# Masked keys as the moving operand, masked blocks filled by DMAs, and the products of a pair of windows in another order

## The reference

```python
q = (x @ wq.T + bq).reshape(B, S, H, D)      # k and v alike
loc = jnp.einsum('bnihd,bnjhd->bnihj', qw, kw) * scale
scores = scores.at[:, n_idx, :, :, n_idx, :].set(loc...)
scores = scores.at[:, gi[:, None], :, gi[None, :]].add(gsc...)
attn = jax.nn.softmax(scores, axis=-1)
out = jnp.einsum('bihj,bjhd->bihd', attn, v).reshape(B, S, HID)
x = _layernorm(x + out @ wo.T + bo)
x = _layernorm(x + ffn(x))                   # argmax of 8 logits picks one 256-64-256 network
```

## Time and profile before

| | |
|---|---|
| median of 3 runs | 444.06 us (442.19 to 445.27) |
| span of the profiled execution | 442.8 us |
| mean granted clock of TensorE | 0.989 |
| busy: PE, PEld, DVE, ACT, POOL | 405.3, 339.8, 326.1, 250.6, 220.4 us |
| row maximum of step 1, of step 5, of step 31 starts at | 39.38, 74.98, 292.66 us |

### The profile page before, as it was taken

The page is one execution under the profiler, slowest core; times in us unless marked ns, Lnnn a source line. Parts: engine busy times, 40 slices in busy tenths (PEclk is TensorE's granted clock), DMA queues, the critical chain, the costliest instruction groups (busy, mean ns, idle before and its releaser), DMA issues.

```text
span 442.8 us, 14658 instructions
## 1 busy us (share of the span) xinstructions
PE 405.3 (92%) x5747; PEld 339.8 (77%) x5747; DVE 326.1 (74%) x796; ACT 250.6 (57%) x523; POOL 220.4 (50%) x301
## 2 busy tenths in 40 slices
PE   5899799999999999999999899988798998999991
PEld 4758678888888888888888778756577887777891
DVE  6785687758757757757759888563668998899785
ACT  3424665675575575575576576676663555544421
POOL 4361343464464464464464566435733485477540
PEclk9999999999999999999999999999989999999997
DMA  8663740000000000000020000000000011011004
GB/s 240 186 199 111 240 137 4 27 25 0 24 24 0 24 24 0 24 24 0 24 72 4 25 2 3 3 1 2 0 2 2 1 49 47 0 47 49 34 15 143
DMA packets 21720, 20.34 MB, mean 46 GB/s; under 512 B 3133, under 2 KB 21682, under 8 KB 21682
## 3 DMA queue, kind: packets, MB, share of 16 engines
q1 hardware_dynamic: 16900, 15.07, 10.9%
q10 hardware_dynamic: 4782, 4.75, 3.3%
HBM read 15.41 MB, written 4.41 MB: 45 GB/s over the span
## 4 chain that ended last, share of the span: by engine, by line
PE 52%; DVE 26%; ACT 9%; issue 8%; DMA 3%; ACTq 1%; DVEq 0%; POOL 0%; POOLq 0%
DVE row_max_t L1154 10%; PE ps L1461 7%; PE ps L1737 7%; PE ps L1424 7%; PE ps L1562 5%; PE ps L1384 5%; PE ps L1415 4%; PE ps L1438 3%; PE ps L1444 3%; ACT probs L847 3%; DVE k_part L1013 2%; ACT boundsT_t L858 2%; PE ps L1406 2%; DMA rows<-in_L_attn_x_dram 2%; ACT k_part L713 2%
## 5 line engine op out<-in xcount | busy, mean ns | idle before, releaser
L847 ACT ACTIVATE probs<-ps 128x1024 f32<-128x1024 f32 x64 | 62.1, 1022 | 68.2 <-PE ps L1428 68.2
L1154 DVE TENSOR_REDUCE row_max_t<-ps 128x16 f32<-128x2048 f32 x31 | 70.9, 2287 | 3.7 <-PE ps L1415 3.6
L1737 PE MATMUL ps<-w_part,hm_part 128*128 128x256 f32 x384 | 53.8, 289 | 1.8 <-DVE hm_part L1332 1.8
L1415 PE MATMUL ps<-k_part,q_part 32*128 32x128 f32 x1584 | 51.5, 274 | 3.1 <-issue 1.5
L1415 PEld LDWEIGHTS ps<-k_part,q_part 32*128 32x128 f32 x1584 | 46.9, 186 | 9.2 <-issue 7.0
L1562 PE MATMUL ps<-xh_parts,w_part 128*128 128x512 f32 x192 | 53.8, 416 | 0.0
L557 POOL TENSOR_TENSOR q_part<-qf,q_part 128x512 fp32r<-128x512 f32 x32 | 41.0, 1281 | 25.7 <-ACT q_part L695 25.7
L599 POOL TENSOR_TENSOR attn_t<-num_t,rden_t 128x256 f32<-128x256 f32 x32 | 20.0, 624 | 64.7 <-DVE rden_t L1185 64.7
L1737 PEld LDWEIGHTS ps<-w_part,hm_part 128*128 128x128 f32 x384 | 48.2, 190 | 4.8 <-DVE hm_part L1332 2.4
L788 ACT ACTIVATE ffn_rows<-ps,b1s 128x512 f32<-128x512 f32 x32 | 22.0, 687 | 42.2 <-PE ps L1562 34.1
L1562 PEld LDWEIGHTS ps<-xh_parts,w_part 128*128 128x128 f32 x192 | 34.7, 194 | 6.5 <-issue 0.6
(11 more groups left out here) (234 smaller groups left out, 906.4 us busy)
## 6 DMA issues: line engine op xcount, KB each, us to landing
table<-rest_sums SPq DMA_DIRECT2D x4, 1088.0 KB, 6.1
xs<-in_L_attn_x_dram SPq DMA_DIRECT2D x16, 256.0 KB, 2.8
rows<-in_L_attn_x_dram ACTq DMA_DIRECT2D x4, 1024.0 KB, 8.1
out_dram<-yout SPq DMA_DIRECT2D x6, 512.0 KB, 2.9
w<-in_L_ffn_W_dram SPq DMA_DIRECT2D x2, 256.0 KB, 7.6
w<-in_L_ffn_W_dram SPq DMA_DIRECT2D x1, 512.0 KB, 4.2
out_dram<-yout SPq DMA_DIRECT2D x2, 256.0 KB, 2.6
out_dram<-yout ACTq DMA_DIRECT2D x2, 256.0 KB, 2.8
```

The costliest lines, as they stand in the source:

```text
L847: act.activation(probs[:, 2 * h:2 * h + 2, :], ps[:, 2 * h:2 * h + 2, :], ACT.Exp).then_inc(probs_ready, 1)
L1154: dve.tensor_reduce(row_max[:], ps_all, op=ALU.max, axis=AX.X).then_inc(max_ready, 1)
L1415: last = mm(ps[:, u, (2 * c + a) * P:(2 * c + a + 1) * P], q_part[x][quad(u), s, c, a, :], k_part[y][quad(u), s, c, :], start=(i == 0), st ...
L1737: mm(y, hm_part[a][:, 1 - p, f, c * P:(c + 1) * P], w2_part[b][:, f, :], start=(f == 0 and i == 0), stop=False)
```

## The change

The masked operand changes sides, and it is no longer computed but copied.

* Even and odd partitions now hold the two heads of a quadrant (weights and biases are put in that order once, at the start). `q_part` and `k_part` are unmasked; `q_apart` and `k_apart` are their masked forms, one for a pair of windows each, with the other head's partitions zero. `k_apart` lies in the tile of the expert layer (`xh_parts`) and is zeroed once by POOL.
* POOL issues two DMAs for each, one for even and one for odd partitions (64 partitions, two runs of 2 KB each): `part_keys` in odd steps, `part_queries` in even steps. There is one buffer of each, so `part_keys` waits for the scores of the pair before, and `part_queries` for its last turned scores.
* `scores(s)` now has the unmasked query stationary and both masked key blocks moving: 24 matmuls of 256 columns. The first two windows and the global tokens keep the old form (`scores_by_queries`).
* Queries are handled as keys are: high part on ACT with bias (two instructions of 128x256), low part on DVE (two). Gone are DVE's four masking instructions, ACT's 128x1024 copy and POOL's `q_low`.
* PE's products move: key product under the even row maximum, query product at the end of the even step; both halves of the values under the odd one; `turn_x` behind the odd turned scores. ACT's and DVE's parts of them move along.

The diff, cut to its core:

```diff
@@ -119,6 +119,8 @@
...
         xh_part = [xh_parts[:, :, i] for i in range(2)]
+        k_apart = xh_parts[:, 0].rearrange("p i c n -> p i (c n)").rearrange("p i (a c w n) -> p i a c w n", a=2, c=KC, w=2)
+        qg_part = xh_parts[:, 1].rearrange("p i c n -> p (i c n)")[:, 0:2 * GT].rearrange("p (i a c n) -> p i a c n", i=2, a=2, c=KC)
...
@@ -551,10 +563,20 @@
...
-            def q_low(w, s):
-                need(pool, turned_scores_in_psum, w - 3)
-                pool.wait_ge(q_high_ready, w // 2 + 1)
-                pool.tensor_tensor(q_part[1][:, s], qf[:, s % 2], q_part[0][:, s].bitcast(fp32), ALU.subtract).then_inc(q_ready, 1)
+            def part_keys(s):
...
+                for a in range(2):
+                    pool.dma_start(k_apart[a:P:2, :, a], k_part[a:P:2, :, s // 2]).then_inc(k_apart_ready, 16)
...
+            def part_queries(s):
...
+                for a in range(2):
+                    pool.dma_start(q_apart[a:P:2, :, a], q_part[a:P:2, :, s // 2]).then_inc(q_apart_ready, 16)
...
+            def first_low(w):
+                pool.wait_ge(q_high_ready, 1)
@@ -572,24 +594,34 @@
...
                 ahead, cur, pp, old, older = (live(t + k, steady) for k in (AHEAD, 0, -2, -3, -4))
+                if live(t + 1, steady) and p:
+                    pool.wait_ge(k_ready, t // 2 + 2)
+                    pool.wait_ge(scores_in_psum, t + 1)
...
                                        e_val[:, p, :].unsqueeze(2).broadcast_to([P, HEADS, VA]), ALU.mult).then_inc(rest_ready, 1)
-                if live(t + 1, steady) and (steady or t > 0):
-                    q_low(t + 1, (s + 1) % SLOTS)
+                if live(t + 1, steady) and p:
+                    if not steady and t == 1:
+                        pool.wait_ge(k_apart_zero, 1)
+                    part_keys((s + 1) % SLOTS)
...
                                        by_quad(bounds[:], 0), ALU.subtract).then_inc(bound_low_ready, 1)
+                    if p == 0 and (steady or t > 0):
+                        pool.wait_ge(q_ready, t // 2 + 1)
+                        pool.wait_ge(turned_scores_in_psum, t)
...
                                        ALU.subtract).then_inc(e_arg_ready, 1)
+                    if p == 0 and (steady or t > 0):
+                        part_queries(s)
...
@@ -635,6 +667,8 @@
...
+            pool.wait_ge(wT_in_psum, 4)
+            pool.tensor_tensor(xh_parts[:, 0].rearrange("p i c n -> p (i c n)"), zeros16[:, 0:1].broadcast_to([P, 4 * GT]), zeros16[:, 0:1].broadcast_to([P, 4 * GT]), ALU.mult).then_inc(k_apart_zero, 1)
...
@@ -723,15 +760,21 @@
...
-                need(act, turned_scores_in_psum, w - 2)
-                act.wait_ge(qf_ready, w // 2 + 1)
-                copy(q_part[0][:, s:s + 2], qf[:]).then_inc(q_high_ready, 1)
+                need(act, turned_scores_in_psum, w - 3)
+                act.wait_ge(q_in_psum, w // 2 + 1)
+                for c in range(KC):
+                    last = act.activation(q_part[:, 0, s // 2, c].rearrange("p w n -> p (w n)"), ps_xq[:, c * 2 * P:(c + 1) * 2 * P],
+                                          ACT.Identity, bias=bq_scaled[:, c:c + 1])
+                last.then_inc(q_high_ready, 1)
...
@@ -808,18 +852,14 @@
...
-                if ahead and p == 0:
-                    turned_x(t + AHEAD)
-                if cur and p == 0 and (steady or t > 0):
-                    values_of(t, s)
+                if not steady and t == 0:
+                    turned_x(AHEAD)
                 if live(t + 1, steady) and p:
-                    keys_of(t + 1, (s + 1) % SLOTS)
+                    queries_of(t + 1, (s + 1) % SLOTS)
...
                     copy(aT[:].rearrange("p c n -> p (c n)"), ps_rao[:, 0:HID]).then_inc(aT_ready, 1)
-                if live(t + 1, steady) and p:
-                    queries_of(t + 1, (s + 1) % SLOTS)
...
                     keep_onehot(0, 0)
+                if live(t + 1, steady) and p:
+                    values_of(t + 1, (s + 1) % SLOTS)
...
                     copy(x_rest[:].rearrange("p c n -> p (c n)"), ps_rao[:, 0:KC * 2 * NW]).then_inc(x_rest_ready, 1)
+                if ahead and p == 0:
+                    keys_of(t + AHEAD, (s + AHEAD) % SLOTS)
+                if live(t + 3, steady) and p:
+                    turned_x(t + 3)
...
@@ -995,44 +1043,53 @@
...
-            def queries_of(w):
...
-                need(dve, q_ready, w)
-                dve.wait_ge(q_in_psum, w // 2 + 1)
+            def first_queries():
...
+                dve.wait_ge(q_in_psum, 1)
...
                     for c in range(KC):
-                        last = dve.scalar_tensor_tensor(qf[:, k, c, :, :],
+                        last = dve.scalar_tensor_tensor(qf[:, :, c, k, :],
                                                         ps_xq[:, (2 * c + k) * P:(2 * c + k + 1) * P].unsqueeze(1).broadcast_to([P, 2, P]),
-                                                        bq_col[:, c:c + 1], q_scale[:], ALU.add, ALU.mult)
-                last.then_inc(qf_ready, 1)
+                                                        bq_scaled[:, c:c + 1], of_half[:], ALU.add, ALU.mult)
+                last.then_inc(q_ready, 1)
...
+            def queries_of(w, s):
...
+                dve.wait_ge(q_high_ready, w // 2 + 1)
+                for c in range(KC):
+                    last = dve.scalar_tensor_tensor(q_part[:, 1, s // 2, c].rearrange("p w n -> p (w n)"), ps_xq[:, c * 2 * P:(c + 1) * 2 * P],
+                                                    bq_scaled[:, c:c + 1], q_part[:, 0, s // 2, c].rearrange("p w n -> p (w n)").bitcast(fp32),
+                                                    ALU.add, ALU.subtract)
+                last.then_inc(q_ready, 1)
...
                 for c in range(KC):
-                    last = dve.scalar_tensor_tensor(k_part[1][:, s:s + 2, c, :], ps_kv[:, c * 2 * P:(c + 1) * 2 * P].rearrange("p (w n) -> p w n", w=2),
-                                                    bk_col[:, c:c + 1], k_part[0][:, s:s + 2, c, :].bitcast(fp32), ALU.add, ALU.subtract)
+                    last = dve.scalar_tensor_tensor(k_part[:, 1, s // 2, c].rearrange("p w n -> p (w n)"), ps_kv[:, c * 2 * P:(c + 1) * 2 * P],
+                                                    bk_col[:, c:c + 1], k_part[:, 0, s // 2, c].rearrange("p w n -> p (w n)").bitcast(fp32),
+                                                    ALU.add, ALU.subtract)
...
@@ -1172,8 +1229,8 @@
...
                 early(1)
-                if ahead and p == 0:
-                    queries_of(t + AHEAD)
+                if live(t + 1, steady) and p:
+                    queries_of(t + 1, (s + 1) % SLOTS)
...
@@ -1211,10 +1268,9 @@
...
                     stack_second_bias(t - 2)
-                if not steady and t == NW - 2:
+                if not steady and t == NW - 1:
...
@@ -1406,27 +1462,37 @@
...
-            def scores(s):
+            def scores_by_queries(queries, keys_):
...
                             for u in range(UNITS):
-                                last = mm(ps[:, u, (2 * c + a) * P:(2 * c + a + 1) * P], q_part[x][quad(u), s, c, a, :],
-                                          k_part[y][quad(u), s, c, :], start=(i == 0), stop=(i == 2), tile_position=(32 * u, 0))
+                                last = mm(ps[:, u, (2 * c + a) * P:(2 * c + a + 1) * P], queries[quad(u), x, a, c, :],
+                                          keys_[quad(u), y, c, :], start=(i == 0), stop=(i == 2), tile_position=(32 * u, 0))
...
-            def turned_scores(s):
+            def both(c, u):
+                return ps[:, u, 2 * c * P:(2 * c + 2) * P].rearrange("p (a n) -> p a n", a=2)
...
+            def scores(s):
...
                         for u in range(UNITS):
-                            mm(ps[:, u, 2 * c * P:(2 * c + 2) * P], k_part[y][quad(u), s, c, :],
-                               q_part[x][quad(u), s, c, :, :].rearrange("p a n -> p (a n)"),
+                            last = mm(both(c, u), q_part[quad(u), x, s // 2, c, s % 2, :], k_apart[quad(u), y, :, c, s % 2, :],
+                                      start=(i == 0), stop=(i == 2), tile_position=(32 * u, 0))
+                return last
...
+            def turned_scores(s):
...
+                for c in range(KC):
+                    for i, (x, y) in enumerate(SPLIT):
+                        for u in range(UNITS):
@@ -1574,9 +1641,15 @@
...
                     need(pe, probs_ready, 2 * (t - 1))
-                    pe.wait_ge(q_ready, t + 1)
-                    pe.wait_ge(k_ready, t // 2 + 1)
-                    scores(s).then_inc(scores_in_psum, 1)
+                    if not steady and t == 1:
+                        pe.wait_ge(first_low_ready, 2)
+                        pe.wait_ge(k_ready, 1)
+                        scores_by_queries(q_apart[:, :, :, :, 1, :], k_part[:, :, 0, :, 1, :]).then_inc(scores_in_psum, 1)
+                    else:
+                        pe.wait_ge(q_ready, t // 2 + 1)
```

(16 more changed lines are left out.)

98 lines of the change are left out of this document (61 added, 37 removed).

## The result

The changed kernel took **450.19 us** (median of 4 runs, 448.74 to 451.91), the one before 444.66 on the same chip (442.19 to 446.3): a ratio of 1.0136, 95% interval 1.009 to 1.0181. The forecast was 441.2, on the other side. The profiled execution (451.49 us, one of the two longer ones) spans 449.4 us against 442.8.

The account below looks back on a forecast made before the run. The prediction took PE, busy 92% of the span, and its ring of handovers with DVE as the bound. Thirteen pairs (-4.3), beginning (+2.0) and end (-0.5) gave -2.8 us, so 441.2 us; range 433 to 455.

Parts of the forecast that it names:

- Scores: PE's score matmuls in each step: 24 of 256 columns in 0.86 us instead of 48 in 1.50, saving 0.64 us.
- Rival 3: Columns, not issue, decide the scores' time, so that edit frees nothing: 458 us; chance 0.05.
- Arc 2: Scores to the next turned scores: 3.49 us in both steps, 0.64 less in odd and 0.54 less in even.
- Arc 1, odd: Turned scores to scores, odd step: turn_x waits for DVE's low queries, 0.85 us more, to 5.16.
- The even arc: Turned scores to scores, even step: query product replaces key product, length kept at 4.45 us.
- POOL's issues: Four DMA issues a pair on POOL: hidden, no cost; the queries' two free up to 0.88 us each.
- Rival 1: POOL's issue of the queries' two DMAs ahead of attn is the bound: 452 us at 1.3 us each; chance 0.22.
- rival 4: The masked copies land late, each us past 4.4 costing one us a pair: 454 us; chance 0.06.
- The pairs: Window loop, steps 5 to 31: each of 13 pairs 0.33 us shorter, 4.3 us in all.
- Beginning: Zero fill of 4.9 us in POOL's queue makes PE 2.4 us late; net +2.0 us, bounds +0.5 and +3.
- End: Two casts move behind the last row maximum and hold up the routing: -0.5 us, bounds -0.9 and +0.5.
- The sum: Whole kernel: -4.3 + 2.0 - 0.5 = -2.8 us, from 444.06 to 441.2 us.

Follow-up runs that it names:

- c_dma4: Changed kernel with fill moved, casts early, square root step removed and earlier key copies; each masked copy split, four POOL issues of 128 KB for two of 256: 450.48 us.
- b_fill: Kernel before the change plus only the zero fill's work on POOL (2048 columns in two instructions, same place): 446.29 us, ratio 1.0049.
- b_take: Kernel before the change with only DVE's casts of the first token group moved from ahead of the last row maximum to behind that step's residual: 447.54 us.
- a_newton: Changed kernel without the reciprocal square root step behind the residual, six early slots a window step instead of seven: 448.16 us.
- d_turn: Changed kernel with one edit, turn_x in odd steps put behind the turned sums and the output product: 442.53 us, ratio 0.9979.

## Why the prediction was wrong, by its own steps

- **Scores: right.** 24 matmuls take 0.92 us (167.85 to 168.77) against the 0.86 forecast and the 1.50 before: 38 ns each. Rival 3 is out, and the row was the better guide. By the rule that the prediction quotes from the Trainium skill (TensorE: Matmul & The Clock Gate, Back-to-back issue gap) the same columns cost nearly the same; here they did not (1.50 and 0.92 us). The same section calls the rule that of an isolated matmul, which counts too little at few columns once weight loads are in the stream; relative to each other the two rows differ that way, though both are shorter than the rule's own sum (some 2.7 us for either, an estimate from it).
- **Arc 2: right.** 171.39 - 167.86 = 3.53 and 179.30 - 175.75 = 3.55, forecast 3.49.
- **Arc 1, odd: right in kind, too large.** Turned 162.93, scores 167.86: 4.93, forecast 5.16. It grew by 0.62 us, not 0.85; VectorE's low queries start 0.36 us behind the turned scores, not 0.49. The other odd step of a round has 3.94 before and 4.54 after, the same 0.6; the prediction drew only the longer one (its pair, 8.44 + 8.48, is 16.92 us and not 16.74). The even arc shrank by 0.05. The chain is the one described, `turn_x` behind VectorE's low queries:

```profile
162.93 0.64 PE L1492 MATMUL ps<-q_apart,k_part 32*128 32x256 f32 x12
...
163.29 0.87 DVE L1060 SCALAR_TENSOR_TENSOR q_part<-ps,qk_bias,q_part 128x256 fp32r<-128x256 f32 x2
...
164.29 0.65 PE L1519 MATMUL ps<-ident,xs 128*128 128x128 f32 x4
...
164.78 0.60 PE L1510 MATMUL ps<-ident,pvT_t 128*128 128x128 f32 x4
```

- **POOL's issues: cost nothing, as forecast, but by luck.** An issue costs 0.63 us, not the 0.37 that was taken from SP's queue; 256 KB land 2.6 us later (forecast 2.8 to 3.8). POOL's own queue, not `rden`, lets `attn` start in the even step: `rden` is there at 174.02, `attn` starts at 174.61. PE turns the attention at 175.44 without a wait, just behind its own query product, so nothing is lost yet and next to nothing is left over (c_dma4).

```profile
173.33 1.26 POOL L574 DMA_DIRECT2D q_apart<-q_part  x2 [0.23 <-issue]
173.77 0.25 DVE L1242 RECIPROCAL rden_t<-num_t 128x16 f32<-128x16 f32 x1
...
174.61 0.64 POOL L631 TENSOR_TENSOR attn_t<-num_t,rden_t 128x256 f32<-128x256 f32 x1
```

  The first issue starts 1.94 us behind the turned scores and not 1.55, so an issue is free up to (3.3 - 1.94) / 2 = 0.68 us, not 0.88. At 0.63 it passed by a hair. Rival 1 did not happen, and rival 4 only once: in step 2 PE waited 2.29 us for the first copies of the keys.
- **The pairs: right for nine, wrong for four.** -0.47 us each over nine steady pairs, forecast -0.33 over thirteen. But steps 23 to 31 are not steady pairs: VectorE has one-off work in steps 24 to 27 and they lost 1.85 us (+3.47, -1.62). From step 5 to 31 the change won 2.4 us where the forecast had 4.3.
- **Beginning: this step failed.** The constants end at 36.9, "PE is 2.4 us late", and a net of +2.0: this priced the fill (4.9 us, measured 3.59) through POOL's own queue, the constants and the bounds. That chain is real (the first low bound came at 35.87, forecast about 37), but PE was not there to wait for it: the longer wait was VectorE's, a subtraction held for 3 us, PE behind it, and then the clock. Only in b_fill does POOL's chain bind, for 1.30 us. Step 5 was 4.65 us late. With the fill elsewhere nothing of it is left.
- **End: this step failed.** "they hold up the routing: -0.5, bounds -0.9 and +0.5" knew the place and the gain (an earlier maximum, 0.86 us in b_take), and put the loss under it. The casts take 1.57 us ahead of the routing, they carry POOL's subtractions with them, those hold two routing instructions for 1.3, and behind PE's wait the clock falls: +4.35 behind the last maximum.
- **The sum:** forecast +2.0 - 4.3 - 0.5 = -2.8 us; in the profiled execution +4.65 up to step 5, -2.40 from there to step 31, +4.35 behind it, +6.6 in all. Of these, 1.6 us at the beginning, 0.6 in step 27 and 1.5 at the end are the clock.
- **The range** held the time (433 to 455), the sign was wrong. No rival had the mechanism: each asked what the moved work costs its own engine.

## What to carry to other kernels

When work is added to or moved on GpSimd, read which VectorE instructions run beside it: those with two SBUF inputs, and wide SBUF-to-SBUF casts, can stand until it is through (0.17 us of work stood 3.10), and each is dear if TensorE waits behind it. Write a fill as a memset: here it took 1.80 us instead of 3.59 and held nothing. Ask also what the work delays on GpSimd's own queue; the longer of the two waits counts. Look at the one-off steps at both ends of a steady loop with the same care as at the loop, because a change worth 0.5 us a pair is lost in two of them; and where a forecast says that an order "gives back most" of a gain, the place of that one step is the next edit to try.

## What was not expected of the hardware

- A VectorE instruction of 20 columns stood 3.10 us through four GpSimd instructions in a row, a cast of 0.67 us stood 3.17; but in the kernel before the same 20 columns took 0.31 beside the same row, in b_fill VectorE came in between two instructions (2.60 us), and so it did for the one-hot. What decides between the row and one instruction is open.
- GpSimd's DMA issue: 0.63 us for 256 KB, 0.55 for 128, and 0.23 in front of the first.
- The granted clock fell behind PE's waits of 2 to 3 us (0.72 from 32 to 38 us after), but not each time: with the same wait of VectorE it held in a_newton and d_turn, 1.6 us apart. At the end it was 0.72 to 0.86, over the 12 us from the one-hot's turning, in each of the eight profiles in which the routing was held, and 1.00 in the eight others.
